# Products of rounded parts first, and unread products in three places, in a 16-sequence decoder layer on one core

## The reference, cut to what matters

```python
x = x + attn_layer(layernorm(x), Wq, Wk, Wv, Wo, omega, W1, b1, W2, b2, gamma, beta)
x = x + cross_attention(layernorm(x), ctx, Wq, bq, Wk, bk, Wv, bv)
x = x + expert_layer(layernorm(x), Wg, W1, W3, W2)      # 16 experts, 2 for each row
```

## Time and profile before

| | |
|---|---|
| median of three runs | 854.63 us |
| the profiled execution | 851.83 us, span of its instructions 850.1 us |
| TensorE busy | 804.8 us (95%) |
| VectorE, ScalarE, GpSimd busy | 610.6, 432.8, 396.1 us |
| mean granted clock of TensorE | 0.983 |
| first product of TensorE | at 7.65 us |
| turns 2 to 14 | about 37.0 to 37.7 us each |
| expert stage | from about 669 us |

### The profile page before, as it was taken

How to read it: one execution, slowest core, us unless ns; L and a number is a source line. 1 busy time by engine, 2 the same in 40 slices (tenths; PEclk the granted TensorE clock), 3 DMA queues, 4 the chain that set the end, 5 groups by cost and what they waited for, 6 DMA issues and landing times.

```text
span 850.1 us, 20930 instructions
## 1 busy us (share of the span) xinstructions
PE 804.8 (95%) x5913; PEld 759.9 (89%) x5914; DVE 610.6 (72%) x1722; ACT 432.8 (51%) x1184; POOL 396.1 (47%) x567
## 2 busy tenths in 40 slices
PE   6889999999999999999999999999988899999991
PEld 5878999999999999999999999999987799999991
DVE  4536788887787888878787877888675566666660
ACT  4235636445462735546273554637243377667661
POOL 3340323435434353543435354343435357777776
PEclk9889999999999999999999999999999999999996
DMA  9537772828466472846647283664399557777770
GB/s 274 193 103 274 273 277 88 298 83 283 131 218 232 156 274 93 292 132 217 234 154 276 86 298 120 229 227 150 134 424 361 150 106 131 120 126 128 123 109 7
DMA packets 105673, 161.19 MB, mean 190 GB/s; under 512 B 10672, under 2 KB 69616, under 8 KB 104752
## 3 DMA queue, kind: packets, MB, share of 16 engines
q1 hardware_dynamic: 79616, 115.62, 41.0%
q0 software_dynamic: 15792, 35.17, 17.5%
q10 hardware_dynamic: 10224, 9.89, 4.2%
HBM read 50.14 MB, written 112.47 MB: 191 GB/s over the span
## 4 chain that ended last, share of the span: by engine, by line
PE 85%; DVE 5%; issue 5%; POOL 2%; ACT 2%; DMA 1%; POOLq 0%; SPq 0%; DVEq 0%; ACTq 0%
PE ps L795 74%; PE ps L806 4%; PE ps L1020 3%; PE ps L1118 2%; PE ps L1140 2%; DVE stat L1450 1%; POOL out L786 1%; DVE attnT_lo L1468 1%; DMA raw_wT<-in_omegaT 1%; DVE xn L1461 0%; POOL rstd L607 0%; POOL expert_rows L678 0%; DVE y L1728 0%; POOLq L101 0%; DVE fT_lo L1468 0%
## 5 line engine op out<-in xcount | busy, mean ns | idle before, releaser
L786 POOL DMA_INDIRECT out<-narrow,sidx x79 | 122.4, 1549 | 53.3 <-DVE sidx L1839 21.4
L795 PE MATMUL ps<-w_hi,fT_hi 128*128 128x256 f32 x256 | 79.4, 310 | 1.1 <-DVE fT_lo L1468 1.1
L1191 ACT ACTIVATE xn3T<-ps 128x512 f32<-128x512 f32 x17 | 10.2, 598 | 136.7 <-issue 108.4
L1468 DVE TENSOR_TENSOR fT_lo<-relu_v,fT_hi 128x512 fp32r<-128x512 f32 x64 | 57.1, 893 | 31.3 <-ACT relu_v L1266 31.3
L1252 ACT ACTIVATE phi<-ps,nmax 128x128 f32<-128x128 f32 x256 | 72.9, 373 | 6.8 <-DVE nmax L1584 6.6
L795 PE MATMUL ps<-hT_hi,w_hi 128*128 128x256 f32 x256 | 73.2, 286 | 1.5 <-DVE hT_lo L1468 1.5
L795 PE MATMUL ps<-hT_hi,w_lo 128*128 128x256 f32 x256 | 72.4, 283 | 0.0
L795 PE MATMUL ps<-hT_lo,w_hi 128*128 128x256 f32 x256 | 72.4, 283 | 0.0
L795 PE MATMUL ps<-w_hi,fT_lo 128*128 128x256 f32 x256 | 72.2, 282 | 0.0
L795 PE MATMUL ps<-w_lo,fT_hi 128*128 128x256 f32 x256 | 72.1, 282 | 0.0
L605 POOL TENSOR_TENSOR veps<-mv,eps_ln 128x2 f32<-128x2 f32 x48 | 10.8, 225 | 129.3 <-DVE mv L1454 129.3
(11 more groups left out here) (297 smaller groups left out, 2853.9 us busy)
## 6 DMA issues: line engine op xcount, KB each, us to landing
expert_rows<-zero_rows SPq DMA_DIRECT2D x16, 4352.0 KB, 15.9
narrow<-expert_rows ACTq DMA_DIRECT2D x71, 136.0 KB
expert_up_hi<-X SPq DMA_DIRECT2D x16, 352.0 KB, 2.8
e_lo<-expert_up_lo POOLq DMA_DIRECT2D x2, 2816.0 KB, 14.1
e_hi<-expert_up_hi POOLq DMA_DIRECT2D x2, 2816.0 KB, 22.2
part_raw<-in_E SPq DMA_DIRECT2D x30, 176.0 KB
expert_up_lo<-part_raw SPq DMA_DIRECT2D x15, 352.0 KB, 3.1
X<-in_x SPq DMA_DIRECT2D x16, 256.0 KB
```

What stands on the lines that cost most here:

```text
L786: pool.indirect_dma_start(out_rows, bass.IndirectOffsetOnAxis(sidx[:, u:u + 1], 0), yg[:, u, :], None, bounds_check=NT * P - 1, oob_is_err ...
L795: return pe.matmul(out_, lhsT, rhs, start=start, stop=stop)
L1191: return act.activation(out_, in_, ACT.Copy)
L1468: dve.tensor_tensor(dst, whole, hi.bitcast(F32), ALU.subtract).then_inc(done, 1)
```

## The change

Three kinds of edit:

1. In `by_token` and `ffn_in`, the products are put in another order: for one PSUM area, first the four products that need only the rounded part of the activations, then the two with their rest. At four places TensorE waits for the rounded part ahead of the first product, and for the rest only ahead of the fifth: `hT` in `ffn_in(0)`, `qT` in the scores (now by `by_token`), `prT` in the attended values and `attnT` in the output projection. Other calls of `by_token` keep their wait ahead of everything.
2. In turn 0, three fillers are added after the transposes of the query features and four after those of the key features, into bank 7.
3. Ahead of the first wait for weights, TensorE issues 17 products of `ones` with `ones` (128 columns, float32) into bank 7, once `ones` and `mask` are set.

```diff
@@ -815,12 +815,18 @@
             def cols(c, lo, n):
                 return (slice(None), c, slice(lo, lo + n))
 
-            def by_token(bank, srcT, w):
+            def by_token(bank, srcT, w, rest_ready=None, value=None):
 
                 for t in range(TS):
+                    to = ps[:, bank, t * D:(t + 1) * D]
                     for c in range(DC):
-                        last = mm3(ps[:, bank, t * D:(t + 1) * D], srcT, w, cols(c, t * P, P), cols(c, 0, D),
-                                   c == 0, c == DC - 1)
+                        at_l, at_r = cols(c, t * P, P), cols(c, 0, D)
+                        mm(to, srcT[0][at_l], w[0][at_r], c == 0, False)
+                        mm(to, srcT[0][at_l], w[1][at_r], False, False)
+                    if t == 0 and rest_ready is not None:
+                        pe.wait_ge(rest_ready, value)
+                    for c in range(DC):
+                        last = mm(to, srcT[1][cols(c, t * P, P)], w[0][cols(c, 0, D)], False, c == DC - 1)
                 return last
 
             def by_feature(bank, srcT, w):
@@ -906,9 +912,15 @@
                 def ffn_in(g, bank):
 
                     for n in range(2):
+                        to, f_cols = ps[:, bank, n * S:(n + 1) * S], (2 * g + n) * P
                         for c in range(DC):
-                            last = mm3(ps[:, bank, n * S:(n + 1) * S], w1, hT, cols(c, (2 * g + n) * P, P),
-                                       cols(c, 0, S), c == 0, c == DC - 1)
+                            at_l, at_r = cols(c, f_cols, P), cols(c, 0, S)
+                            mm(to, w1[0][at_l], hT[0][at_r], c == 0, False)
+                            mm(to, w1[1][at_l], hT[0][at_r], False, False)
+                        if g == 0 and n == 0:
+                            pe.wait_ge(hT_ready, f + 1)
+                        for c in range(DC):
+                            last = mm(to, w1[0][cols(c, f_cols, P)], hT[1][cols(c, 0, S)], False, c == DC - 1)
                     last.then_inc(w1_ps, 1)
 
                 if a is not None:
@@ -949,7 +961,7 @@
 
                         pe.wait_ge(split_lo, N_DVE_SPLIT)
                         pe.wait_ge(pool_split_lo, N_POOL_SPLIT)
-                    pe.wait_ge(hT_ready, f + 1)
+                    pe.wait_ge(hT_hi, f + 1)
                     ffn_in(0, 2)
                     ffn_in(1, 3)
                 if b is not None:
@@ -957,12 +969,8 @@
                         pe.wait_ge(v2_ready, b + 1)
                     if last_cross:
                         keep_clock(2, 3)
-                    pe.wait_ge(qT_ready, b + 1)
-                    for t in range(TS):
-                        for c in range(DC):
-                            last = mm3(ps[:, 7, t * S:(t + 1) * S], qT, ctx, cols(c, t * P, P), cols(c, 0, S),
-                                       c == 0, c == DC - 1)
-                    last.then_inc(score_ps, 1)
+                    pe.wait_ge(qT_hi, b + 1)
+                    by_token(7, qT, ctx, qT_ready, b + 1).then_inc(score_ps, 1)
                 def count_choices():
 
                     if a is not None:
@@ -1024,15 +1032,19 @@
 
                 if a is not None:
                     turn_phi(0, qpT_ps)
+                    if first(i):
+                        keep_clock(7, 3)
                     turn_phi(2, kpT_ps)
+                    if first(i):
+                        keep_clock(7, 4)
                 if f is not None and not last_ffn:
                     ffn_out(1, 0, 2)
                 if last_cross:
                     keep_clock(2, 4)
                 if b is not None:
-                    pe.wait_ge(prT_ready, b + 1)
+                    pe.wait_ge(prT_hi, b + 1)
                     pe.wait_ge(v2_ready, b + 1)
-                    by_token(6, prT, v2).then_inc(av_ps, 1)
+                    by_token(6, prT, v2, prT_ready, b + 1).then_inc(av_ps, 1)
                 if last_cross:
                     count_choices()
                 if a is not None:
@@ -1078,11 +1090,14 @@
                 if b is not None and not last_ffn:
                     router(b, 6)
                 if a is not None:
-                    pe.wait_ge(attnT_ready, a + 1)
-                    by_token(3, attnT, wo).then_inc(wo_ps, 1)
+                    pe.wait_ge(attnT_hi, a + 1)
+                    by_token(3, attnT, wo, attnT_ready, a + 1).then_inc(wo_ps, 1)
                 if first(i):
                     score_weights()
 
+            pe.wait_ge(blank, 2)
+            for _ in range(17):
+                mm(ps[:, 7, 0:P], ones[:, :], ones[:, :])
             pe.wait_ge(fuse_loaded, 16 * 3)
             pe.wait_ge(const_ready, N_CONST)
             fuse(0)
```

## The result

The changed kernel takes 852.21 us in the median of 20 runs (850.16 to 855.18), the kernel before 855.03 on the same chip (851.74 to 859.19): ratio 0.9963, 95% interval 0.995 to 0.9975, that is 3.2 us less (2.1 to 4.3). The profiled execution took 850.57 with a span of 848.8; the one of before had 851.83 and 850.1. One execution each differs by 1.3 us, which is less than either kernel's own spread; so the profiles are read for their instants, and the times for the verdict.

What follows compares the result with a forecast made beforehand. A steady turn was taken as a ring through VectorE, without the output projection. Terms -1.2 - 1.7 - 0.7 - 0.5 = -4.1 us gave 847.7 profiled, 850.5 median; own range 849.3 to 851.8, with both neighbours 846.6 to 853.4.

Steps and rivals of the forecast that it cites:

- both neighbours: The rivals beside the forecast: projection waits come back in every turn (13%, 846.5), the start gives back its gain (17%, 852.6).
- the start gives back its gain: Rival, 17%: the clock falls again, bk ends with xwv_lo, or a low stretch grows; -2, some 852.6 us.
- (a): 17 products of ones at the start: value products at 14.0, scores at 28.0 instead of 29.21; -1.2 us.
- (b): Turn 0's fillers of three and four: they keep the clock up for the score products; -1.7 us.
- the third of its ways: Third cause named for that rival: the low-clock stretch after turn 0's bias products grows.
- (c): Turn 0's output projection: its 1.41 us wait shrinks as four high-part products go 0.74 earlier; -0.7 us.
- (d): Turn 1's w1 products: four go ahead during the 1.50 us wait for hT_lo; -0.5 us, bounds -0.4 and -0.7.
- (e): All other turns: projection starts up to 0.5 us earlier, TensorE then waits for xn2T_lo; 0, other bound -4.
- the ring: Steady turn's loop: attnT_lo, fixed VectorE row, xn2T_lo, TensorE's long stretch, transposes of attn, attnT_hi, attnT_lo; output projection outside it.
- rival of 0.3 us in every turn: Rival, 13%: the gain of the waits at the projection comes back in every turn, 4 us more; 846.5 us.

Runs made afterwards that it cites:

- e10: The changed kernel as it is, run again for a second profile: 852.14 us, ratio 0.9949 to the kernel before.
- e7: The changed kernel without the seven unread products of constants in turn 0, ones and new orders kept: 837.14 us on the second chip, ratio 0.9974 to before.
- e2: The kernel before with only the 17 products of ones and turn 0's seven unread products, old orders: 853.91 us, ratio 0.9998 to before.
- e3: The changed kernel with one more unread product of constants ahead of the transposes of z in turns 2 to 15: 851.41 us, ratio 0.9968 to before.
- e4: The changed kernel with GpSimd's copy of xn held until VectorE has written z: 846.08 us, ratio 0.9903 to before.
- e1: The changed kernel without the 17 products of ones and turn 0's seven unread products, new orders kept: 852.98 us, ratio 0.9977 to before.
- e9: The changed kernel with GpSimd's copy of xn held until z is written and four unread products among turn 0's bias products: 845.01 us, ratio 0.9881 to before.
- e12: As e9, but with the product orders of the kernel before: 850.84 us, ratio 0.9938 to before.
- e6: The changed kernel without the 17 products of ones, turn 0's unread products and new orders kept: 839.27 us on the second chip, ratio 1.0004 to before.
- e5: The kernel before with only GpSimd's copy of xn held until z is written: 836.82 us on the second chip, ratio 0.9976 to before.

## Why the prediction was right, and where not

The time was forecast at 850.5 and is 852.2: inside the range with both neighbours (846.6 to 853.4) and on the right side, but outside the forecast's own 849.3 to 851.8, and 0.4 from the 852.6 of the rival that the start gives back its gain. Against before, which came out 0.4 higher than in the prediction, it was -4.1 forecast and -3.2 measured. By its steps:

- (a) Right in place, a little small in size: value products at 14.03, scores at 27.73 for 28.0. "GpSimd's work hangs on transfers and stays where it is" was wrong: it went from 21.85 to 20.38. And "the second `bk` row as done there", with `w2_lo`, was wrong in this execution: both rows were over at 26.38, 0.1 behind `xwv_lo` (25.03 + 1.27 = 26.30), as before. The two errors cancel, which is luck. In after, e10 and e7 the rows end with `xwv_lo`, in e2, e3 and e4 with `w2_lo`.
- (b) The scores' 1.7 us were there in the first pair, and the cover for the seven products too. The term that failed is the last: "where in it the clock falls again is between -0.8 and +0.8". From numerators to `attnT_lo` it was +2.4 (12.8 against 10.4), and in all five profiles of the new start between +0.8 and +2.4. And before's own low scores came in one profile of two, so their price was half a property of the execution. (a), (b) and the clock together were forecast at -2.9. At the numerators the means over the nine profiles have just that; at turn 1's value products, less (c), -1.8 is left, with -1.2 between the first profiles of before and after and +0.3 between the second; e2's time says -0.2 (-1.7 to +1.4). This is the rival "the start gives back its gain", by the third of its ways, and in part.
- (c) Right: forecast -0.7, measured 1.41 to 0.69, in e1 as well.
- (d) Forecast -0.5, measured 1.50 to 0.78: the whole 0.7 us of the VectorE instruction, the upper bound.
- (e) Right, and for its reason. The wait moved to `z`, `y` didn't move (3.23 us behind `attnT_lo` in turn 8's start, 3.22 in the earlier trace rows), the turn stayed at 37.0, a further product there cost 0.03 us (e3), and 0.57 us a turn came out as soon as the ring was shortened elsewhere (e4, e9 against e12). The rival of 0.3 us in every turn is out for this kernel; for one with an early `z` it is true, with 0.57.

So the size of the sum was right in part by luck. (c) and (d) brought 1.4 us where 1.2 were forecast, and e1, which has only them, measured -2.0 (-3.4 to -0.5). The start, by the nine profiles, brought some 1.8 at turn 1 and 1.4 at turn 2's `xn2T_lo` (with (d) taken out too) where 2.9 were forecast. Together that is -2.8 to -3.2; the whole change measured -3.2, and -4.4 the second time (-6.5 to -2.3). The 1.8 is a difference of means of five and four single executions that differ by up to 2.7 and 1.5 us among themselves, so it is an estimate. By the times alone the start's share is open: e2's interval ends at -1.7, and the whole change is 1.2 to 2.4 beyond e1.

## What to carry to other kernels

Where two engines pass work around a loop, read what the consumer waits for after the wait that you remove. If the same interval is set by another engine's fixed row, the edit is worth nothing until that row is shorter too; so test the pair, not each alone. A clock stretch that is won in one place can be lost in the next: follow it until the clock's last rise before the steady part, and look at what the engine did before each fall; a busy row isn't proof that the clock stays. And take a second profile of the kernel before, ahead of pricing a stretch in which the clock is low; where the clock differs between executions, compare several profiles of a start, not one pair.

## What the runs showed of the hardware

- 16 score products took 4.52 us in one execution of the kernel before and 2.85 in another, with a clock that fell in the one and not in the other.
- 17 products of ones (34 records, 6.47 us from 1.58) had the clock at 2.4 GHz for the weight products at 7.98. Without them (e6) the weight products, 64 rows by 128 columns, ran at 1.2 GHz (3.78 us for each 16), and so did what followed without pause, until about 21.4: records of `wq` and `wk` are 0.43 us apart up to there and 0.23 behind.
- Two VectorE instructions of 128x256 took 1.78 us beside GpSimd's copy and addition, and 0.72 without them. The same copy and addition beside `xn2T_lo` and `v_lo`, which read PSUM, left these at 0.69 and 0.68 (e4). The `bk` rows, two of 128x128, took 3.27.
- In all eleven profiles without unread products among turn 0's bias products the clock fell there and stayed low for 10.2 or 13.6 us; in the three with them it stayed at 2.4 GHz.
- On the first chip `attnT_hi` starts on ScalarE 28.2 us after `xn2T_lo` (28.5 to 28.6 in e4, e9 and e12), and in 1 to 6 of 13 turns 0.7 later; each such turn is 0.65 longer. In two turns of the kernel after, one long and one not, the transposes ahead of it start 27.15 and 27.16 us after `xn2T_lo`, `attnT_hi` 28.89 and 28.26. Two long turns are not of this kind: in e1's turn 5 and e10's turn 7 the row from `attnT_lo` to `xn2T_lo` takes 9.59 and 8.70 for 8.2. On the second chip `attnT_hi` starts at 27.85 (28.24 in e5) in all but a few turns. Six such turns are 4 us of an execution; what delays ScalarE's start, no view shows.
